# Two layers of attention and experts on one core: the latent inputs of batches 1 to 7 are made inside the perceiver instead of in a stage of their own

## What is computed

```python
x = x + L0_xattn(layernorm(x), ctx, ctx, mask0, ...)
x = x + L0_ffn(layernorm(x), ...)      # slots: alpha @ slot_values, then @ wo + bo
x = x + L1_xattn(ctx, layernorm(x), mask1, ...)
x = x + L1_ffn(x, ...)                 # the best of 8 experts for each token
```

```python
q = ln @ Wq
k, v = split(concatenate((xn, ln), axis=1) @ Wkv)
attn = softmax(where(mask, q @ k.T, max_neg))     # 16 heads of 64
out = layernorm((attn @ v) @ Wout)
```

## Time and profile before

| | |
|---|---|
| median of three runs | 2923.05 us |
| the profiled execution | 2921.61 us |
| its span, first to last instruction | 2919.8 us |
| mean granted TensorE clock | 0.953 |
| latents' stage | 828 to 1000 us of the span |
| perceiver | 1000 to about 2490 us |

### The profile page before, as it was taken

How to read it: one execution, slowest core, us unless ns; L and a number is a source line. 1 busy time by engine, 2 the same in 40 slices (tenths; PEclk the granted TensorE clock), 3 DMA queues, 4 the chain that set the end, 5 groups by cost and what they waited for, 6 DMA issues and landing times. The chain is left out here.

```text
span 2919.8 us, 41005 instructions
## 1 busy us (share of the span) xinstructions
PE 2646.1 (91%) x14566; PEld 2188.7 (75%) x14566; DVE 2023.6 (69%) x4005; ACT 1517.6 (52%) x2897; POOL 1522.0 (52%) x1149
## 2 busy tenths in 40 slices
PE   6699999986778699999999999999999998799698
PEld 5577777763436588888888888888888887677476
DVE  3677777742546377777777777777777777577666
ACT  2234334331213277777777777777777777111175
POOL 2355544320000166666666666666666666465555
PEclk9899999998878899999999999999999999899899
DMA  5212222133348633334333343233433314668475
GB/s 188 56 54 56 56 57 57 41 96 128 139 145 312 228 74 80 106 83 115 81 77 109 80 118 81 75 111 76 122 80 77 109 51 136 210 238 288 157 275 187
DMA packets 212526, 351.15 MB, mean 120 GB/s; under 512 B 75839, under 2 KB 82370, under 8 KB 204631
## 3 DMA queue, kind: packets, MB, share of 16 engines
q1 hardware_dynamic: 193539, 284.89, 32.8%
q0 software_dynamic: 11680, 45.02, 4.2%
q10 hardware_dynamic: 7104, 18.61, 1.6%
HBM read 172.47 MB, written 156.64 MB: 113 GB/s over the span
## 5 line engine op out<-in xcount | busy, mean ns | idle before, releaser
L1880 POOL TENSOR_SCALAR pa_Pr<-pa_Pr,pa_rs 128x590 f32<-128x590 f32 x512 | 902.4, 1769 | 485.1 <-DVE pa_rs L2109 484.9
L2113 DVE TENSOR_REDUCE pa_least<-pa_S 128x1 f32<-128x590 f32 x512 | 390.7, 763 | 230.0 <-PE pa_S L1944 227.9
L2034 ACT ACTIVATE pa_Pr<-pa_S,pa_least 128x590 f32<-128x590 f32 x512 | 385.5, 753 | 99.4 <-DVE pa_least L2113 96.0
L2066 DVE TENSOR_TENSOR pa_PTl<-pa_W,pa_PTh 128x512 fp32r<-128x512 f32 (+1 forms) x640 | 421.2, 684 | 20.5 <-ACT pa_PTh L2005 16.4
L2005 ACT ACTIVATE pa_PTh<-pa_W 128x512 fp32r<-128x512 f32 (+1 forms) x640 | 367.0, 596 | 58.4 <-PE pa_W L1955 47.1
L1955 PE MATMUL pa_W<-pa_ident,pa_Pr 128*128 128x128 f32 (+1 forms) x2560 | 369.7, 275 | 0.6
L1955 PEld LDWEIGHTS pa_W<-pa_ident,pa_Pr 128*128 128x128 f32 (+1 forms) x2560 | 302.4, 142 | 30.0 <-POOL pa_Pr L1880 2.8
L1971 PE MATMUL pa_O<-pa_PTh,pa_V 128*128 128x512 f32 (+1 forms) x640 | 289.2, 452 | 18.6 <-DVE pa_PTl L2066 14.4
L1972 PE MATMUL pa_O<-pa_PTl,pa_V 128*128 128x512 f32 (+1 forms) x640 | 253.4, 396 | 0.0
L1942 PE MATMUL pa_S<-pa_U,pa_Qh 128*128 128x296 f32 (+1 forms) x1024 | 228.9, 305 | 7.5 <-ACT pa_Pr L2034 0.5
L1942 PEld LDWEIGHTS pa_S<-pa_U,pa_Qh 128*128 128x128 f32 x1024 | 183.2, 188 | 55.5 <-ACT pa_Pr L2034 21.3
(11 more groups left out here) (503 smaller groups left out, 6545.6 us busy)
## 6 DMA issues: line engine op xcount, KB each, us to landing
xs_s<-pa_Ql SPq DMA_DIRECT2D x57, 576.0 KB
pa_Um<-pa_U SPq DMA_DIRECT2D x128, 147.5 KB
pa_Qh<-pa_Qh SPq DMA_DIRECT2D x128, 128.0 KB
o_s<-pa_O_hi SPq DMA_DIRECT2D x64, 256.0 KB, 2.0
o_s<-pa_O_lo SPq DMA_DIRECT2D x64, 256.0 KB, 2.3
Wkv_hi<-o_s SPq DMA_DIRECT2D x8, 2048.0 KB, 11.3
Wkv_lo<-o_s SPq DMA_DIRECT2D x8, 2048.0 KB, 17.0
l_xa<-x SPq DMA_DIRECT2D x8, 1024.0 KB, 6.5
```

The source lines that it names most:

```text
L1880: pool.tensor_scalar(p, p, rs[:, g % 2, t:t + 1], None, ALU.mult).then_inc(*pool_s.mark("probs", n))
L2034: act.activation(Pr[g % 2][:, t, :], scored[n % 2], ACT.Exp, scale=-1.0, bias=least[:, g % 2, t:t + 1], accum_out=rs[:, g % 2, t:t + 1]).t ...
L2066: dve.tensor_tensor(out, src, f32(hi_ap), ALU.subtract).then_inc(*dve_s.mark(*name))
L2113: dve.tensor_reduce(least[:, g % 2, t:t + 1], scored[n % 2], AX, ALU.min).then_inc(*dve_s.mark("least", n))
```

## The change

In the latents' stage only batch 0 keeps its latent input (`FIRST = 1`); the keys of the eight pairs and the ten units of values are made as before, one pair after another. Batches 1 to 7 are made in the perceiver, 28 tiles of 128 tokens. The tiles of batch b start at the steps 64 (b - 1) + 0, 12, 24 and 36, and are spread from there: at -2 ScalarE's queue loads x1 and alpha (and vo, for a batch's first tile); at -1 VectorE writes alpha's row of ones; at 0 TensorE does the residual product; at 1 VectorE adds and measures; at 2 GpSimd makes variance and power, and ScalarE's queue stores x2; at 3 VectorE normalises; at 4 TensorE transposes, four into one bank; at 5 VectorE applies gain and bias, four operations of 128 columns; at 6 ScalarE copies the high part; at 7 VectorE subtracts the low part and the high part is stored; at 8 the low part is stored. Residual product and transposes claim one of the three banks W. One buffer for x and one for the norm serve all tiles. SyncE's load of a batch's z waits for the stores of its four tiles.

Beside it: the low part of the output is written over the sum (`O`), so the next copy of sums waits for the output's stores; ScalarE's high part of the output and GpSimd's low part move from t = 2 to t = 1; the mask's words lie in the norm's buffer; GpSimd sets one more constant.

```diff
-    RING = 3
+    RING, FIRST = 1, 1
...
-        batch = lambda b: 0 <= b < B
+        batch = lambda b: 0 <= b < FIRST
...
-            load_small(1)
-            load_x(2)
-            for b in range(B):
+            for b in range(FIRST):
                 sp.wait_ge(*dve_s.after("free", "x2", b, NT - 1))
-                sp.dma_start(x2_s[b:b + 1].rearrange("b (t p) d -> p (b t) d", p=P), X[b % RING]).then_inc(x2_out[b % RING], 16)
-                if batch(b + 2):
-                    load_small(b + 2)
-                if batch(b - 1):
-                    for q, h in [i for i in v_of(b - 1) if i[1]]:
-                        values_out(q)
-                    keys_out(b - 1)
-                if batch(b + 2) and b > 0:
-                    load_x(b + 2)
-            for q, h in [i for i in v_of(B - 1) if i[1]]:
-                values_out(q)
-            keys_out(B - 1)
-            for r in range(RING):
-                sp.wait_ge(x2_out[r], 16 * len(range(r, B, RING)))
+                sp.dma_start(x2_s[b:b + 1].rearrange("b (t p) d -> p (b t) d", p=P), X[b]).then_inc(x2_out[b], 16)
+            for b in range(PAIRS):
+                keys_out(b)
+                for q, h in [i for i in v_of(b) if i[1]]:
+                    values_out(q)
+            for b in range(FIRST):
+                sp.wait_ge(x2_out[b], 16)
             for m in range(2):
                 sp.wait_ge(K_out[m], 16 * PAIRS)
...
             context()
-            for b in range(B):
-                if batch(b + 1):
-                    read_out(b + 1)
+            for b in range(FIRST):
                 transposed(b)
+            for b in range(PAIRS):
                 keys(b)
...
 
-            for b in range(B):
+            for b in range(FIRST):
                 latents(b)
+            for b in range(PAIRS):
                 for h in range(2):
                     act.wait_ge(*pe_s.after("K", b, h))
                     if b >= 2:
                         act.wait_ge(K_out[b % 2], 32 * (b // 2))
                     act.activation(Kst[0][b % 2][:, h * HALF:(h + 1) * HALF], bank_of["K", b, h][:, 0:HALF], ACT.Copy)\
                        .then_inc(*act_s.mark("hi", "K", b, h))
-                low_out(b)
+                if batch(b):
+                    low_out(b)
                 for k, h in v_of(b):
                     act.wait_ge(*pe_s.after("V", k, h))
                     if k:
                         act.wait_ge(V_out, 16 * k)
                     src, hi, _ = v_parts(k, h)
...
-                    dve.wait_ge(*pe_s.after("zT", b - 1, C - 1))
                 for t in range(NT):
                     dve.tensor_scalar(xn[:, t, :], X[r][:, t, :], mv[m][:, t, 0:1], rstd[m][:, t:t + 1],
                                       ALU.subtract, ALU.mult).then_inc(*dve_s.mark("xn", b, t))
-                if batch(b + 1):
-                    add_and_measure(b + 1)
...
                 for c in range(C):
                     dve.wait_ge(*act_s.after("hi", b, c))
                     dve.tensor_tensor(z_lo[m][:, c, :], full[m][:, c, :], f32(z_hi[m][:, c, :]), ALU.subtract).then_inc(*dve_s.mark("lo", b, c))
+            for b in range(PAIRS):
...
         ident = sb("ident", [P, P])
-        mask_words = sb("mask_words", [1, B * SK // 4], I32)
-        mask_u = mask_words[:, :].bitcast(mybir.dt.uint8)
+        lx, ln = sb("x_next", [P, D]), sb("xn_next", [P, D])
+        l_hi = lx[:, :].bitcast(F32R)
+        alphas = ln[:, 0:P]
+        vo = sb("vo", [NS + 1, D])
+        lp = sb("norm", [P, 2 * C + 11])
+        gain = [lp[:, n * C:(n + 1) * C] for n in range(2)]
+        lstats, lmv = lp[:, 2 * C:2 * C + 6], lp[:, 2 * C + 6:2 * C + 8]
+        lve, lrstd, minus_half = (lp[:, 2 * C + 8 + n:2 * C + 9 + n] for n in range(3))
+        mask_words = ln[0:1, 0:B * SK // 4].bitcast(I32)
+        mask_u = mask_words.bitcast(mybir.dt.uint8)
         z = pair("z", [P, C, T])
         U = [two(f"U{m}", [P, Z], F32R) for m in range(2)]
...
         PTh, PTl = (sb(n, [P, RING, T], F32R) for n in ("PTh", "PTl"))
-        O = sb("O_sum", [P, T])
...
+        APART = 3 * NT
+        tiles = [(b, t) for b in range(1, B) for t in range(NT)]
+        begins = {STEPS // B * (b - 1) + APART * t: i for i, (b, t) in enumerate(tiles)}
+        tile_at = lambda n, late: begins.get(n - late)
...
+                if b:
+                    sp.wait_ge(z_out, 32 * NT * b)
                 for n in range(2):
                     sp.dma_start(f32(z[n][:, :, :]), z_s[n][b:b + 1].rearrange("b p c z -> p (b c) z")).then_inc(z_in, 16)
 
...
                 sp.wait_ge(*pool_s.after("O lo", p))
                 for n in range(2):
-                    sp.dma_start(o_s[n][p // BP, p % BP], f32(Os[n][:, :])).then_inc(o_out, 16)
+                    sp.dma_start(o_s[n][p // BP, p % BP], (f32(Os[0][:, :]), O[:, :])[n]).then_inc(o_out, 16)
 
...
+            pool.memset(minus_half, -0.5).then_inc(setup, 1)
...
+                if t == 1 and g >= 3 and g % 2 == 1:
                     low_part((g - 3) // 2)
+                i = tile_at(n, 2)
+                if i is not None:
+                    pool.wait_ge(*dve_s.after("x2 var", i))
+                    pool.tensor_scalar(lve, lmv[:, 1:2], 1.0 + EPS, EPS * EPS, ALU.mult, ALU.add).then_inc(*pool_s.mark("x2 ve", i))
+                    pool.wait_ge(*pool_s.after("x2 ve", i))
+                    pool.tensor_tensor(lrstd, lve, minus_half, ALU.pow).then_inc(*pool_s.mark("x2 rstd", i))
             low_part(PAIRS - 1)
 
         @block.tensor
...
-            pe.wait_ge(setup, 20)
+            def residual(i):
+                u = ("x2", i)
+                claim(u)
+                pe.wait_ge(x_in, 32 * (i + 1))
+                pe.wait_ge(vo_in, 16 * (i // NT + 2))
+                pe.wait_ge(*dve_s.after("ones", i))
+                pe.matmul(bank_of[u][:, :], alphas[0:NS + 1, :], vo[:, :], start=True, stop=True).then_inc(*pe_s.mark(*u))
+                release(u)
+
+            def latent(i):
+                u = ("zT", i)
+                claim(u)
+                pe.wait_ge(*dve_s.after("xn", i))
+                for c in range(C):
+                    m = pe.transpose(bank_of[u][:, c * P:(c + 1) * P], ln[:, c * P:(c + 1) * P], ident[:, :])
+                m.then_inc(*pe_s.mark(*u))
+                release(u)
+
...
                     value(q, j)
+                if tile_at(n, 0) is not None:
+                    residual(tile_at(n, 0))
+                if tile_at(n, 4) is not None:
+                    latent(tile_at(n, 4))
 
         @block.scalar
...
 
+            def fetch(i):
+                b, t = tiles[i]
+                if i == 0:
+                    act.wait_ge(mask_row, 2)
+                    act.dma_start(vo[NS:NS + 1, :], a["L0_ffn_bo"].rearrange("(o n) -> o n", o=1)).then_inc(vo_in, 16)
+                else:
+                    act.wait_ge(z_out, 32 * i)
+                act.dma_start(lx[:, :], x1_s[b, t * P:(t + 1) * P, :]).then_inc(x_in, 16)
+                act.dma_start(alphas[0:NS, :], alphaT_s[b][:, t * P:(t + 1) * P]).then_inc(x_in, 16)
+                if t == 0:
+                    if i:
+                        act.wait_ge(*pe_s.after("x2", i - 1))
+                    act.dma_start(vo[0:NS, :], vo_s[b]).then_inc(vo_in, 16)
+
+            def keep(i):
+                b, t = tiles[i]
+                act.wait_ge(*dve_s.after("read", "x2", i))
+                act.dma_start(x2_s[b, t * P:(t + 1) * P, :], lx[:, :]).then_inc(x2_out, 16)
+
+            def latent_out(z, i):
+                b, t = tiles[i]
+                src = (lx, ln)[z][:, :].rearrange("p (c k) -> p c k", c=C)
+                act.dma_start(z_s[z][b][:, :, t * P:(t + 1) * P], src).then_inc(z_out, 16)
+
+            for dst, name in zip(gain, ("L1_xattn_ln_l_g", "L1_xattn_ln_l_b")):
+                act.dma_start(dst, a[name]).then_inc(norm_in, 16)
             for n in range(1 - LEAD, STEPS + 2 * NT + 1):
                 g, t = divmod(n, NT)
...
                     if x == 0 and p > 0:
-                        act.wait_ge(*pool_s.after("O lo", p - 1))
+                        act.wait_ge(o_out, 32 * p)
                     copy(O[x * HD:(x + 1) * HD, :], Oc[(1 - x) * HD:(2 - x) * HD, :], "low", g - 2)
                 if t == 1:
                     probabilities(g - 1, 0)
                     probabilities(g - 1, 1)
-                if t == 2:
                     if head(g - 2) and g % 2 == 1:
                         p = (g - 2) // 2
                         act.wait_ge(*dve_s.after("O", g - 2))
                         if p > 0:
                             act.wait_ge(o_out, 32 * p)
                         act.activation(Os[0][:, :], O[:, :], ACT.Copy).then_inc(*act_s.mark("O hi", p))
+                if t == 2:
                     probabilities(g - 1, 2)
                     probabilities(g - 1, 3)
                 if t == 3:
                     probabilities(g - 1, 4)
+
+                if tile_at(n, -2) is not None:
```

(51 more changed lines are left out.)

57 lines of the change are left out of this document (21 added, 36 removed).

## The result

Four runs of the changed kernel took 2979.33, 2966.99, 2966.19 and 2979.71 us, median **2973.16**, against 2923.64 before (four runs too): ratio 1.017, 95% interval 1.0135 to 1.0206. The forecast was 2965 within 2915 to 3000, slower. The four lie in two groups, 13 us apart; the profiled run is the one of 2979.33, of the upper group. Sign and size were right; two terms were not, and their errors partly cancel.

A forecast was written before the change was run, and what follows sets the result against it. TensorE, busy 1287 of 1304 us in the perceiver, was taken as the bound there: 2921.6 + 90 for the tiles - 47 given back by the latents' stage = 2964.6, so 2965 us, range 2915 to 3000.

The forecast's parts named there:

- the three stalls that were named: Perceiver, tiles from position 4: T2 behind sum and statistics, VectorE's normalisation behind GpSimd's power, query product behind the scaled copies.
- The stage: Latents' stage: moving seven batches out gives back 47 us, bounds 33 to 75; last values issued at 946, not 991.
- At the stage's 0.88, 65: Latents' stage: remaining keys and values take TensorE 57 us at full clock, 65 at the stage's granted clock of 0.88.
- bank turnovers of 13 with store waits of 7: Latents' stage: keys and values sharing two banks cost 13 us of waits, the values' single buffer awaiting its stores 7.
- TensorE's floor: Perceiver: product 0.86 and transposes 0.40 make 1.26 us a tile, uncovered, 35 us for 28 tiles.
- Tiles at position 4: Perceiver, 14 tiles starting at step 4 of a head pair's eight (0 to 7): 1.7 + 0.7 + 0.4 + 1.6 = 4.4 us each.
- T2 late: Perceiver, tiles from position 4: transposed unit T2 of position 6 comes 1.7 us later, 0.86 product and 0.85 stall.
- Tiles at position 0: Perceiver, 14 tiles starting at the first of a head pair's eight score steps: 2.0 us each.
- the third load: Perceiver, a batch's first tile: one load more and the least room, two steps ahead; no time put down.
- Output stores: Perceiver: they gate the next copy of sums instead of GpSimd's low part, which comes one step earlier; no cost put down.
- VectorE's slack: Rival, perceiver: VectorE's 22% idle time absorbs the chain, a tile costs its 1.26 us, total 2910; chance 0.15.
- Blocked SBUF operations: Rival, perceiver: a tile's two-input SBUF subtraction waits up to 1.77 us for GpSimd's product; total 3000, chance 0.14.

The follow-up runs named there:

- e4: The change with the tiles' residual product and transposes issued but their banks read by nobody, the rest of the tile arithmetic left out, transfers kept: 2906.89 us.
- e5: The change with GpSimd's variance and power of a tile issued ahead of its product of probabilities, not behind it: 2958.83 us.
- e2: The change with tiles started 13 steps apart, so that each of the 16 positions of two head pairs has one or two (the scan): 3014.84 us.

## Why the prediction was right, and where its steps were not

The mechanism was right: the stage gave back what its remaining work allows, and a tile in the full pipeline costs more than TensorE's own work, by the three stalls that were named. That the total came within 9 us of 2965 is in part luck: 13 us too little were taken for the stage and 25 too little for the perceiver.

**The stage: mechanism right, 13 us too small.** Keys began 30.7 us behind the stage's first transfer (862.02 - 831.37), where 859.5 meant 30.9. From there the last value store was to come at 946; by the same clock it came at 933.4 (936.23 less the 2.8 of the later start). Two terms were mis-sized. "At the stage's 0.88, 65": TensorE was busy 59.6, at 0.96, for the clock of a stage full of chains was taken over to one with fewer. And bank turnovers of 13 with store waits of 7: TensorE waited 13.6 for both, because only one of the three value stores held it (3.9 at most). The next stage follows 6.3 us behind the last store, not 8.7: the 2 taken, 2.4 measured.

**TensorE's floor: 35 forecast, about 25.** "Nothing covers this: TensorE has no gaps" was the step that failed, and behind it the reading that each row "starts where the last one's columns end, so the 99% is real": the 0.37 us in which the scores of position 6 waited for the exponential are mostly covered by a busy row of 1.03. At position 4 the product cost 0.35 in e4, not 0.86, and the transposes of a tile from position 0, which fall on the same place, 0.07, not 0.40. Elsewhere both cost about what was forecast: the product 1.0 at position 0, the transposes 0.44 behind a start at 4.

**Tiles at position 4: 4.4 forecast, 3.9.** By step: T2 late 1.4 (forecast 1.7), GpSimd's power 1.3 (0.7; e5 takes 1.0 away), transposes and the query's wait 1.2 (2.0). The scaled copies were estimated at 0.286 each; the row has 0.40 alone, and four together 1.35, but they start sooner, so the wait is 0.93 on the mean.

**Tiles at position 0: 2.0 forecast, 2.15 to 2.6 undisturbed, 47.6 in all where 28 was taken.** In five of the six dear ones a late transfer stands in the trace: in three TensorE waits for the third load, in two ScalarE's copy waits for an output store; the sixth shows neither. "Loads are issued two steps ahead, 4 us or more, against 3.9 for a whole megabyte; the batch's first tile has a third load and the least room" named the place and put down nothing; TensorE waited four times for that third load, 5.2 us in all.

**Output stores: put down at nothing, cost 16.1 us in the steps.** "Output stores now gate the next copy of sums instead of GpSimd's low part, which itself comes one step earlier" stated the new wait, but did not ask what stands ahead of the store on SyncE's queue in the last pair. Behind the steps 4.8 us come back.

**The rivals.** VectorE's slack did not take up the chain: the two ways parted at 0.42 us of stall a tile, and even at the best position of the scan a tile costs 1.4 over TensorE's 0.9. Blocked SBUF operations: the last subtraction, with two inputs in SBUF, ran 680 to 684 ns in all 28 tiles, and in 13 of them the first 0.58 us lie inside a product of GpSimd. One such pair, GpSimd and VectorE in order of time:

```profile
1651.57 1.78 POOL L1868 TENSOR_SCALAR pa_Pr<-pa_Pr,pa_rs 128x590 f32<-128x590 f32 x1
1652.77 0.68 DVE L2195 TENSOR_TENSOR pa_xn_next<-pa_xn_next,pa_x_next 128x512 f32<-128x512 f32 x1
```

That product took its usual 1.77 too. The exclusive lock of the Trainium skill's page "SBUF — State Buffer", section "Who interferes with whom", does not show in this pair, where the measurement decides; the 7.04 us of the earlier trace rows beside four two-input sums of GpSimd agree with it. e2 has both cases with one and the same subtraction. In its four tiles at position 7 it starts just behind GpSimd's low part of the output, which has two inputs in SBUF, and takes 1.62 to 1.75 us (GpSimd, then VectorE):

```profile
1112.05 1.28 POOL L1862 TENSOR_TENSOR pa_O_sum<-pa_O_sum,pa_O_hi 128x512 f32<-128x512 f32 x1
1112.13 1.75 DVE L2195 TENSOR_TENSOR pa_xn_next<-pa_xn_next,pa_x_next 128x512 f32<-128x512 f32 x1
```

In the other 24 it takes 0.67 to 0.69, and nine of these begin inside GpSimd's product, which has one tensor as input. So the rival's block exists in this kernel, beside GpSimd's two-input operation; beside the product, which the prediction had in mind, it does not occur.

## What to carry to other kernels

In a pipeline whose first engine is full, the price of inserted work is set by its place: the same tile cost 2.3 to over 6 us by the step at which it started, and one run with the starts spread over all positions read out the whole table. Price the two halves of a piece of work apart, each where it stands. Read gaps from the starts of the rows and not from the busy share, which hid a wait of 0.37 us here. And when a buffer is merged to save room, follow its new releaser to its queue and look at what stands ahead of it at every irregular point: the end, and the change of a batch. A store moved forward brings its own wait along, and what stands behind it in that engine's order waits too.

## What was not expected of the hardware

TensorE's granted clock in the latents' stage was 0.88 before, 0.96 in the change with its fewer waits, and 1.00 once values had banks of their own. So three banks gave 17.3 us: the waits of 13.6, and 3.7 of busy time (59.62 to 55.88 for the same 316 products). A subtraction of VectorE with both inputs in SBUF ran beside a one-tensor product of GpSimd without loss (0.68 us, 13 times), and beside GpSimd's subtraction of two tensors it took 1.62 to 1.75 us (four times). And moving two loads to another engine's queue did not make a store of the first queue land sooner (16.1 us of waits against 16.0), with the DMA engines 97% busy at one such place.
